# A decoder layer's attention rows through HBM: k rows stored once and read as three blocks, q rows written in three parts

## The chip, the cores and the metric

The kernel runs on one NeuronCore of one Trainium2 chip. The time is device microseconds of one execution; the kernel before was timed three times, with a median of 647.1 us (646.86 to 648.7). Everything shown here from inside an execution comes from one more, profiled execution. In this text TensorE (the matrix engine) is PE, VectorE is DVE, ScalarE is ACT and GpSimd is POOL; SP is the engine that issues nearly all DMAs.

## The reference, cut to what matters

The input is 16 batches of 128 rows of 128 features. Three blocks follow one another, each with 16 heads of 8 features: causal self-attention without projections, cross-attention with a bias of 16x16x128x128, and an attention block with a mixture of experts behind it.

```
def reference(x, ctx_1024, bias, ...):
    # self-attention: q = k = v = layernorm(x)
    w = einsum('bhqd,bhkd->bhqk', q, k) / sqrt(8);  w = where(causal, w, min)
    x = x + merge(softmax(w) @ v)
    # cross-attention: q from layernorm(x), k and v from ctx_1024
    scores = einsum('bhtd,bhsd->bhts', q, k) + bias
    x = x + merge(softmax(scores) @ v) @ Wo.T + bo
    # third block, on x = layernorm-ed input: attention with wq, wk, wv, wo,
    # then layernorm, argmax over 8 experts, relu(h @ w1[e] + b1[e]) @ w2[e] + b2[e]
    ...
```

## The kernel before, in words

The three layers (SELF, CROSS, FFN in the code) go over the 16 batches in pairs of two, so there are 24 pairs in all, numbered 0 to 23 here (SELF 0 to 7, CROSS 8 to 15, FFN 16 to 23). One head has only 8 features, and q and k are wanted to nearly float32 accuracy from bfloat16 matmuls. So q and k of a pair are each split into three bfloat16 parts (high, middle, low), and the product of all nine combinations of parts is one matmul with 9 x 8 = 72 rows: the tile `stack` holds on its 72 partitions the q rows (index 0) and the k rows (index 1) of a pair, for all 16 heads, 8192 bytes per row. Row r of q and row r of k must be the same feature, and over the 9 rows of a feature every q part meets every k part once.

The parts come out of ACT and POOL in the tile `parts`, whose partition is head by feature. To bring the features onto the partitions the rows go through scratch tensors in HBM:

- `write_parts` (L323) waits until POOL has written the low part (L501) and until the stack reads that used the same scratch buffer are done, and then issues one DMA of the q rows (L330, 192 KB) and three of the k rows (L335, 192 KB each). Each k DMA writes one part to three places, so `k_scratch` holds all 72 rows of k (576 KB); `q_scratch` holds 24 rows.
- `read_stack` (L338) waits until all four have landed (`WRITES`, L204) and until the first score group of the pair before is computed, so that the other stack buffer is free. Then it issues one DMA of the q rows (L346, every scratch row read three times) and one of the 72 k rows (L349).

SP works through its list in order. In each pair it reads the stack of the next pair, loads bias tiles (CROSS, `load_bias`, L351) and context rows (L364), and, one batch later, writes the parts of the pair after. `scores` and `score_maxes` on PE wait for the stack (semaphore `s_stack`); in CROSS and FFN `score_maxes` of the next pair is the first to do so, in the first batch of the pair before. All this runs through DMA queues that SP feeds. Behind the three layers come the routing and the 23 expert tiles, which the change does not touch.

## Time and profile before

| | us |
|---|---|
| median of 3 runs | 647.1 |
| the profiled execution | 649.13 |
| its span, first to last instruction | 647.4 |
| PE busy | 474.6 (73% of the span) |
| DVE busy | 295.2 (46%) |
| ACT busy | 216.3 (33%) |
| PE waiting for the stack rows (matmul side) | 88.1 |

The span is 1.7 us shorter than the execution's time. The three attention layers fill the first 500 us, the routing and the experts the rest. PE's busy time is a sum over overlapping matmuls, so 73% does not say that PE is the limit; what counts is where PE stands still and who ends the stillness.

### The profile page before, as it was taken

Reading aid. Unit: us, or ns where it says so; the run is one execution under the profiler, and the core shown is the slowest. Engines: PE = TensorE matmul, PEld = TensorE weight load, DVE = VectorE, ACT = ScalarE, POOL = GpSimd, SP = SyncE. Lnnn points to the kernel's source line nnn. Section 1 sums busy time; section 2 is a strip of 40 time slices with the busy share of each in tenths; the row PEclk is TensorE's granted clock in tenths of the full one; section 3 lists DMA queues with packets and bytes.
Section 4 is the critical chain, followed back from the end, with each engine's and each line's share of the span. In section 5 each row is a group of like instructions: output and inputs, shape, how many; then the busy total and the mean of one; then the engine's idle time right before and its main releaser. Section 6 shows DMA issues by size and latency. Waiting matters only on the chain.

```text
span 647.4 us, 15191 instructions
## 1 busy us (share of the span) xinstructions
PE 474.6 (73%) x4957; PEld 351.0 (54%) x4958; DVE 295.2 (46%) x1230; ACT 216.3 (33%) x415; POOL 131.2 (20%) x223
## 2 busy tenths in 40 slices
PE   0369669668988988987976956875785982058886
PEld 0246446446767777776765644554564761026664
DVE  4013223235756766675745635544544444014443
ACT  1136346433333343333233532432433330013331
POOL 4301112101011011111112111211202131713333
PEclk9968789768989999998979978967977555569999
DMA  6874565727687679575314224313328930222220
GB/s 181 235 191 114 162 170 136 190 73 175 153 196 181 163 185 222 150 184 139 86 38 123 57 68 121 95 46 103 107 53 230 345 120 0 106 69 53 72 67 19
DMA packets 95613, 83.82 MB, mean 129 GB/s; under 512 B 4934, under 2 KB 88905, under 8 KB 91993
## 3 DMA queue, kind: packets, MB, share of 16 engines
q1 hardware_dynamic: 94072, 80.20, 47.3%
q0 software_dynamic: 1504, 3.16, 1.4%
q8 instruction: 20, 0.33, 0.2%
q14 instruction: 17, 0.13, 0.1%
HBM read 58.29 MB, written 25.51 MB: 129 GB/s over the span
## 4 chain that ended last, share of the span: by engine, by line
PE 38%; DMA 24%; issue 17%; DVE 7%; POOL 6%; SPq 4%; ACT 2%; DVEq 0%; POOLq 0%; ACTq 0%
DMA stack<-k_scratch 19%; PE score_bank L582 13%; PE out_bank L582 7%; DMA k_scratch<-parts 4%; PE finish_bank L582 4%; PE prep_bank L582 3%; PE max_bank L582 3%; POOL routed_rows L559 2%; PE finish_bank L585 2%; SPq L335 2%; PE score_bank L585 2%; SPq L346 2%; PE max_bank L585 1%; POOL parts L501 1%; PE prep_bank L585 1%
## 5 line engine op out<-in xcount | busy, mean ns | idle before, releaser
L911 ACT ACTIVATE probs<-score_bank 128x512 f32<-128x512 f32 x192 | 115.0, 599 | 201.0 <-PE score_bank L582 200.7
L582 PE MATMUL score_bank<-stack 72*128 72x128 bf16 x768 | 143.1, 237 | 1.2 <-DVE maxT L1115 0.5
L582 PE MATMUL score_bank<-maxT,pick 128*128 128x128 bf16 x512 | 98.2, 230 | 0.0
L582 PE MATMUL max_bank<-stack 72*128 72x128 bf16 x512 | 55.5, 246 | 56.8 <-DMA stack<-k_scratch 56.1
L582 PE MATMUL out_bank<-probs,vaug 128*32 128x128 f32 x1536 | 90.1, 311 | 2.6 <-DVE vaug L1081 1.8
L582 PEld LDWEIGHTS score_bank<-stack 72*128 72x128 bf16 x768 | 83.6, 110 | 13.1 <-issue 8.8
L1093 DVE CUSTOM_DVE_ANT_0 max_bank<-max_bank,bias_in 128x128 f32<-128x128 f32 x256 | 66.2, 324 | 46.7 <-PE max_bank L582 46.2
L582 PEld LDWEIGHTS max_bank<-stack 72*128 72x128 bf16 x512 | 37.8, 109 | 72.3 <-issue 42.1
L1098 DVE TENSOR_REDUCE rowmax<-max_bank 128x4 f32<-128x512 f32 x64 | 43.4, 689 | 63.0 <-PE max_bank L582 62.7
L582 PE MATMUL score_bank<-causal,identb 128*128 128x128 bf16 x256 | 44.0, 249 | 32.0 <-DMA stack<-k_scratch 32.0
L501 POOL TENSOR_TENSOR parts<-rest,parts 128x512 bf16<-128x512 f32 (+1 forms) x24 | 23.9, 994 | 213.3 <-ACT parts L903 213.3
L585 PE MATMUL score_bank<-ident,bias_in 128*128 128x128 f32 x256 | 65.8, 290 | 1.0 <-DVE maxT L1115 0.2
L582 PEld LDWEIGHTS score_bank<-maxT,pick 128*128 128x128 bf16 x512 | 53.4, 104 | 3.4
L582 PEld LDWEIGHTS score_bank<-causal,identb 128*128 128x128 bf16 x256 | 27.2, 111 | 47.6 <-issue 47.3
L475 POOL TENSOR_SCALAR vareps<-meanvar 128x2 f32<-128x2 f32 x40 | 8.7, 218 | 210.8 <-DVE meanvar L1026 210.8
L1122 DVE RECIPROCAL rowsum_inv<-finish_bank 128x16 f32<-128x16 f32 x48 | 12.3, 256 | 80.1 <-PE finish_bank L585 80.1
L582 PEld LDWEIGHTS out_bank<-probs,vaug 128*32 128x32 f32 x1536 | 31.9, 114 | 28.9 <-issue 11.9
L585 PE MATMUL finish_bank<-ident,outT 128*128 128x128 f32 x203 | 37.4, 305 | 7.7 <-ACT outT L917 7.6
L585 PEld LDWEIGHTS score_bank<-ident,bias_in 128*128 128x128 f32 x256 | 36.6, 143 | 10.6 <-issue 6.5
L1303 DVE TENSOR_TENSOR probs<-score_bank,b_rows 128x512 f32<-128x512 f32 x23 | 15.9, 692 | 47.9 <-PE score_bank L582 47.9
L1093 DVE DVE_READ_ACCUMULATOR2_ANT rowmax<- 128x1 f32 x256 | 36.4, 142 | 0.0
L582 PE MATMUL finish_bank<-wxo,att_sel 128*128 128x128 f32 x256 | 34.9, 294 | 1.0 <-DVE att_sel L1129 0.5
(135 smaller groups left out, 706.9 us busy)
## 6 DMA issues: line engine op xcount, KB each, us to landing
bias_in<-in_bias SPq DMA_DIRECT2D x32, 512.0 KB, 9.1
k_scratch<-parts SPq DMA_DIRECT2D x72, 192.0 KB, 2.9
stack<-q_scratch SPq DMA_DIRECT2D x24, 576.0 KB
stack<-k_scratch SPq DMA_DIRECT2D x24, 576.0 KB
q_scratch<-parts SPq DMA_DIRECT2D x24, 192.0 KB, 2.7
routed_rows<-filler SPq DMA_DIRECT2D x1, 2955.5 KB, 20.4
w<-in_w SPq DMA_DIRECT2D x1, 2048.0 KB, 23.9
b_rows<-in_b SPq DMA_DIRECT2D x1, 2048.0 KB, 20.2
```

The source lines that it names most:

```text
L335: sp.dma_start(k_rows, parts[:, i, part, wk, :].unsqueeze(1).to_broadcast([128, NT, PAIR])).then_inc(s_wr[i], 16)
L346: sp.dma_start(stack[:, i, 0, :, :], q_src).then_inc(s_stack[i], 16)
L475: nc.gpsimd.tensor_scalar(vareps[:], meanvar[:, :, 1], EPS, None, ALU.add).then_inc(s_ve, 1)
L501: nc.gpsimd.tensor_tensor(parts[:, i, 2, 0:n, :], rest[:, 0:n, :], parts[:, i, 1, 0:n, :], ALU.subtract).then_inc(s_lo, 1)
L559: nc.gpsimd.indirect_dma_start(out=routed, out_offset=bass.IndirectOffsetOnAxis(ap=position_i[:, n:n + 1], axis=0), in_=rows_out[:, n, :], ...
L582: return nc.tensor.matmul(o, lhsT, rhs, start=start, stop=stop, **kw)
L585: return nc.tensor.matmul(o, src, ident[:], start=True, stop=stop, is_transpose=True)
L911: nc.scalar.activation(probs[:, g, :], sbk[g % 2][:], ACT.Exp, scale=1.0 if st.layer == CROSS else SCALE).then_inc(s_p, 1)
L1093: last = nc.vector.tensor_tensor_reduce(out=bank[:, h * S:(h + 1) * S], in0=bank[:, h * S:(h + 1) * S], in1=bias_in[:, k % 4, head, :], sc ...
L1098: last = nc.vector.tensor_reduce(rowmax[:, g * G:(g + 1) * G], bank[:].rearrange("p (h k) -> p h k", h=G), AX.X, ALU.max)
L1122: nc.vector.reciprocal(rowsum_inv[:], o[:, :, HD]).then_inc(s_inv, 1)
L1303: nc.vector.tensor_tensor(mid[:, k % 2, :], sbk[k % 2][:], b1_rows[:, bass.ds(e, 1), :].rearrange("p o f -> p (o f)"), ALU.add).then_inc(s ...
```

## The change

`k_scratch` loses the dimension that repeated each row three times: it has 24 rows (192 KB) now, feature by part, and one DMA writes them. `q_scratch` is ordered part by feature, so its rows are written by three DMAs of 64 KB, one per part. On the way back the q rows are still read by one DMA, each row three times in a row; the 24 k rows are read three times, by three DMAs, each into one block of 24 stack partitions. The number of stack rows and what stands on them in pairs is the same, in another order. So a pair writes 384 KB instead of 768 KB, and reads 1152 KB as before; it takes 8 DMA issues instead of 6.

```diff
-        q_scratch = nc.dram_tensor("q_scratch", (2, HD, NT, NH, PAIR), bf16, kind="Internal").ap()
-        k_scratch = nc.dram_tensor("k_scratch", (2, HD, NT, NT, NH, PAIR), bf16, kind="Internal").ap()
+        q_scratch = nc.dram_tensor("q_scratch", (2, NT, HD, NH, PAIR), bf16, kind="Internal").ap()
+        k_scratch = nc.dram_tensor("k_scratch", (2, HD, NT, NH, PAIR), bf16, kind="Internal").ap()
...
-        WRITES, READS = (1 + NT) * 16, 2 * 16
+        WRITES, READS = (1 + NT) * 16, (1 + NT) * 16
...
-                q_rows = bass.AP(tensor=q_scratch.tensor, offset=q_scratch[i].offset,
-                                 ap=[[PAIR, NH], [row_elems, HD * NT], [1, PAIR]])
-                sp.dma_start(q_rows, parts[:, i, :, 0, :]).then_inc(s_wr[i], 16)
                 wk = 0 if st.layer == SELF else 1
                 for part in range(NT):
-                    k_rows = bass.AP(tensor=k_scratch.tensor, offset=k_scratch[i, 0, 0, part].offset,
-                                     ap=[[PAIR, NH], [NT * row_elems, HD * NT], [1, PAIR]])
-                    sp.dma_start(k_rows, parts[:, i, part, wk, :].unsqueeze(1).to_broadcast([128, NT, PAIR])
-                                 ).then_inc(s_wr[i], 16)
+                    q_rows = bass.AP(tensor=q_scratch.tensor, offset=q_scratch[i, part].offset,
+                                     ap=[[PAIR, NH], [row_elems, HD], [1, PAIR]])
+                    sp.dma_start(q_rows, parts[:, i, part, 0, :]).then_inc(s_wr[i], 16)
+                k_rows = bass.AP(tensor=k_scratch.tensor, offset=k_scratch[i].offset,
+                                 ap=[[PAIR, NH], [row_elems, HD * NT], [1, PAIR]])
+                sp.dma_start(k_rows, parts[:, i, :, wk, :]).then_inc(s_wr[i], 16)
...
                 k_src = bass.AP(tensor=k_scratch.tensor, offset=k_scratch[i].offset,
-                                ap=[[row_elems, ROWS], [1, row_elems]])
-                sp.dma_start(stack[:, i, 1, :, :], k_src).then_inc(s_stack[i], 16)
+                                ap=[[row_elems, HD * NT], [1, row_elems]])
+                for rep in range(NT):
+                    sp.dma_start(stack[rep * HD * NT:(rep + 1) * HD * NT, i, 1, :, :], k_src).then_inc(s_stack[i], 16)
```

On PE, DVE, ACT and POOL the list of instructions is the same. SP's list at the start of the program, as a difference (a DMA's shape is its destination's, x3 is three of them; L358 are the first bias tiles):

```order
 L320 DMA gate_w<-in_gate_w 128x8
 L321 DMA gate_b<-in_gate_b 128x8
-L330 DMA q_scratch<-parts 16x24x256
-L335 DMA k_scratch<-parts 16x24x256 x3
-L346 DMA stack<-q_scratch 72x1x4096
-L349 DMA stack<-k_scratch 72x4096
+L332 DMA q_scratch<-parts 16x8x256 x3
+L335 DMA k_scratch<-parts 16x24x256
+L345 DMA stack<-q_scratch 72x1x4096
+L349 DMA stack<-k_scratch 24x4096 x3
```

Nothing has moved past anything else here: the four writes are one large one and three small ones now, the large one last, and two more reads stand before what follows. The same in the last step of SELF, where the context and bias loads of CROSS begin:

```order
 L364 DMA ctx_in<-in_ctx 128x2x128 x2
-L346 DMA stack<-q_scratch 72x1x4096
-L349 DMA stack<-k_scratch 72x4096
+L345 DMA stack<-q_scratch 72x1x4096
+L349 DMA stack<-k_scratch 24x4096 x3
 L358 DMA bias_in<-in_bias 128x8x128 x2
```

The bias loads come behind two more DMA issues.

## Rows read from the trace of the kernel before

**Rows 1.** Page, part 4: the chain that ended last, by line, share of the span.

```profile
DMA stack<-k_scratch 19%; PE score_bank L582 13%; PE out_bank L582 7%; DMA k_scratch<-parts 4%; PE finish_bank L582 4%; PE prep_bank L582 3%; PE max_bank L582 3%; POOL routed_rows L559 2%; PE finish_bank L585 2%; SPq L335 2%; PE score_bank L585 2%; SPq L346 2%; PE max_bank L585 1%; POOL parts L501 1%; PE prep_bank L585 1%
```

**Rows 2.** Waits: who waited for whom; us in total, times, longest us.

```profile
PE max_bank L582 <- DMA stack<-k_scratch: 56.1, 16, 6.9
PE score_bank L582 <- DMA stack<-k_scratch: 32.0, 5, 12.7
```

**Rows 3.** PE in order of time: start, us, what, [idle before, releaser].

```profile
161.35 0.61 PE L582 MATMUL max_bank<-stack 72*128 72x128 bf16 x8 [0.48 <-DMA stack<-k_scratch]
...
209.24 0.61 PE L582 MATMUL max_bank<-stack 72*128 72x128 bf16 x8 [1.21 <-DMA stack<-k_scratch]
...
424.48 1.04 PE L582 MATMUL max_bank<-stack 72*128 72x128 bf16 x8 [5.36 <-DMA stack<-k_scratch]
```

**Rows 4.** The chain, 194 to 210 us (pair 11): start, us, what.

```profile
194.53 1.17 POOL parts L501
...
195.72 0.56 SPq L330
...
196.33 0.62 SPq L335
...
197.68 2.88 DMA k_scratch<-parts
...
200.68 0.82 SPq L346
...
201.54 7.57 DMA stack<-k_scratch
...
209.24 0.61 PE max_bank L582 x8
```

**Rows 5.** SP's DMA issues by line: count, duration ns min/median/max, first and last start.

```profile
L330 SPq DMA_DIRECT2D q_scratch<-parts x24: 546/556/1128, 10.7 to 481.9; - x24
...
L335 SPq DMA_DIRECT2D k_scratch<-parts x72: 615/641/955, 11.4 to 483.8; - x72
...
L349 SPq DMA_DIRECT2D stack<-k_scratch x24: 516/528/540, 18.2 to 487.5; - x24
...
L407 SPq DMA_DIRECT2D outT<-routed_rows x23: 328/333/787, 570.6 to 629.4; - x23
```

**Rows 6.** Page, part 6: count, KB each, median us from issue to landing.

```profile
k_scratch<-parts SPq DMA_DIRECT2D x72, 192.0 KB, 2.9
...
q_scratch<-parts SPq DMA_DIRECT2D x24, 192.0 KB, 2.7
```

**Rows 7.** Stretches of the span; the last two columns are DMA share and GB/s.

```profile
core 0: us, PE busy (x) PEld busy (x) DVE busy (x) ACT busy (x) POOL busy (x), PEclk, DMA share, GB/s
...
372.20:378.00 5.80, 0.00 (x0) 0.00 (x0) 0.77 (x3) 0.00 (x0) 0.92 (x3) 0.84 0.69 189
...
203.00:208.00 5.00, 4.94 (x61) 3.71 (x59) 2.45 (x11) 2.40 (x5) 1.47 (x4) 1.00 0.90 233
...
435.50:438.70 3.20, 2.85 (x40) 1.85 (x39) 2.75 (x11) 0.68 (x2) 0.00 (x0) 1.00 0.95 243
504.00:512.00 8.00, 7.46 (x54) 6.25 (x55) 3.52 (x9) 3.02 (x6) 1.52 (x3) 0.50 1.07 357
```

**Rows 8.** The chain, 12 to 42 us (pairs 0 and 1): start, us, what.

```profile
12.77 4.54 DMA k_scratch<-parts
...
18.21 7.66 DMA stack<-k_scratch
...
31.34 10.34 DMA stack<-k_scratch
```

**Rows 9.** SP in order of time, 18 to 31 us: start, us, what.

```profile
21.45 8.08 SPq L358 DMA_DIRECT2D bias_in<-in_bias  x4
29.87 1.42 SPq L346 DMA_DIRECT2D stack<-q_scratch  x1
```

**Rows 10.** PE's weight loads in order of time, at 106.5 us (pair 6).

```profile
106.50 0.10 PEld L582 LDWEIGHTS score_bank<-causal,identb 128*128 128x128 bf16 x1 [0.26 <-DMA stack<-k_scratch]
```

## The prediction

> **What bounds the kernel now.** I read the chain of waits first. Its largest single piece is no engine but a transfer: the stack rows' read has 19% of the span and the writes of the k rows 4% [rows 1]. The list of waits says the same from PE's side: PE stood still 56.1 us, 16 times, before the row maxima of a new pair, and 32.0 us, 5 times, before scores, each time for the stack's read [rows 2]. In order of time one sees how long each such stop is: 0.48 us at pair 9, 1.21 us at pair 11, 5.36 us at pair 20; the other CROSS and FFN pairs lie between 1.2 and 6.9 us [rows 3]. So in nearly every pair PE is done early, and what sets the pair's length is a loop: POOL's low part, SP's four write issues, the last k write's landing, the two read issues, their landing, PE's work until the next low part [rows 4]. From the landing to the next low part PE works without a stop, so a microsecond less between the low part and the landing is a microsecond less per pair, until PE's stop is used up.
>
> The read is not late for another reason: the first score group of the pair before, the read's other wait, is ready some 5 us before the read's issue in pairs 9 to 23 and in 3, 5 and 7, by the start of the exponentials that follow it. In pairs 2, 4 and 6 it comes 1 us before the issue, about with the landing, so there the writes have nothing to give.
>
> **The writes.** Before, the first issue starts at 195.72 and the last of four at 197.68, 1.96 us later; it lands after 2.88 us more, so 4.84 us from first issue to last landing [rows 4]. Now three issues of 64 KB come first, and one of 192 KB last. No row shows the small one. The bounds are 0.33 us (a plain 64 KB load late in the program) and 0.64 us (the repeated k write) [rows 5]; I take 0.48, nearest to the q write's 0.556, whose shape it shares with a third of the pieces. With the gaps of 0.05 us that stand between issues, the k write is issued 3 x 0.53 = 1.6 us after the first. A 192 KB write with nothing queued in front landed in 2.7 us, the ones behind it in 2.9 [rows 6]. Sum 4.3 us, so **0.55 us gained** per pair. The ends: 3 x 0.38 + 2.7 = 3.8 us (1.0 gained) and 3 x 0.69 + 2.9 = 5.0 us (0.1 lost). The halved bytes by themselves give little here: SP's issues pace the writes, and the engines are only just behind (243 GB/s at a share of 0.95 [rows 7]).
>
> **The reads.** The q read is unchanged. The k read is three DMAs of 24 rows, with as many bytes and as many rows of 8192 bytes. Issuing three takes 2 x (0.53 + 0.05) = 1.15 us longer [rows 5], but issue is not what the read waits for: from the k issue to the landing it is 7.57 us [rows 4], in which 1152 KB go at 189 GB/s with a share of 0.69 [rows 7], so the q rows alone keep the engines busy for about 3 us and the last k issue comes 2 us after the first read issue, in time. What it costs depends on what the 189 GB/s are limited by. A stretch in which bias tiles are loaded beside the read has 233 GB/s, and the experts' weights came with 357 [rows 7], so it is neither the HBM nor the engines as a whole; the rate belongs to this transfer, to its 72 rows. With 24 rows at a time it may be the same or lower. The low end is no cost, or 0.3 us gained (192 KB of source instead of 576; the landings vary by as much). The high end is far: 10.34 us was measured for a k read in company of bias loads, 2.7 us above the 7.66 of the one before [rows 8]. I take **0.5 us lost** per read, nearer to the low end since bytes, rows and the order in which engines get them stay, and under half of the 1.15 us by which the last issue moves.
>
> The Trainium skill has a rule that speaks against the change: in "SBUF — State Buffer", section "Door 1: The DMA port swizzle", a transfer's rate is the number of ports that its partitions reach times 27.2 GB/s, and partitions 0 to 63 reach only eight of sixteen. By it 24 partitions reach six ports, an estimate of 163 GB/s, 3.6 us for 589,824 bytes. The 189 GB/s of the 72 rows [rows 7] fit its eight ports and a little, so the trace agrees as far as it goes; the k half takes 3.1 us at 189 GB/s, the rule's cost is 0.5 us, and no row here shows a transfer to 24 partitions.
>
> **The sum.** Pairs 3, 5, 7, 8 and 9 to 23 have both terms on the path: 19 x (-0.55 + 0.5) = -1.0 us. Pair 9, with a stop of 0.48, can't give more than that, which the sum does not feel.
>
> At the start the writes of pair 0 queue behind the weights' loads: their last landing takes 4.54 us instead of 2.9 [rows 6, 8]. Here the bytes count: 384 KB less at 243 GB/s is 1.6 us, less 0.5 for the read: -1.1. Pair 1's read stands behind four bias issues, which take 8.08 us since their queue is full of pair 0's read and pair 1's writes [rows 9]; the same bytes leave that queue, the same 0.5 is paid: -1.1 again.
>
> Pairs 2, 4 and 6 have their read released by PE, and its landing is just in time (a weight load of pair 6 stood 0.26 us for it [rows 10]). They pay the 0.5 us less a small slack: I take 0.2 each, +0.6. Bias and context loads come 1.15 us later from SP. Their cover is that a bias tile is asked for three batches ahead; without it PE would lose that 1.15 us at most once per pair.
>
> Total -1.0 - 2.2 + 0.6 = **-2.6 us**. The profiled execution took 649.13 us, 2.0 above the median of 647.1, so I take the difference off the median: **644.5 us**. The own range of this case, with the per-pair net between -0.35 and +0.3, is 638 to 650. A measurement of this kernel can tell about 0.3%, 1.9 us, from no change.
>
> **The rivals.**
> 1. The read is not slower at all. Speaking for it: same bytes, same number of rows, queue never empty. Against: that the rate belongs to the 72 rows, which become 24. Then 19 x -0.55 = -10.5, at the start -3.2, pairs 2, 4, 6 nothing: -13.7, about 633.5 us. Chance 0.22.
> 2. Slower: the three blocks of 24 rows go at three quarters of the present rate, 142 instead of 189 GB/s, so the k half takes 4.1 instead of 3.1 us. The point from which it decides is a cost of 0.65 us per read. Then 19 x (1.0 - 0.55) = +8.6, pairs 2, 4, 6 with 0.8 each +2.4, the start -1.2: +9.8, 657 us. For it: a third of the partitions, and the loss falls on every pair's loop. Against: the engines still have the same rows each. Chance 0.24.
> 3. The writes give nothing: the small q writes cost 0.64 us each in SP like the k writes, so the last is issued at 2.07 us instead of 1.96, and lands as late as before. For it: the issue cost in the rows does not follow the bytes (0.53 us for 576 KB, 0.64 for 192 [rows 5]). With 0.5 us for the read: +9.5, the start -1.0, the rest +0.6: +9, 656 us. Chance 0.12.
>
> **How the numbers follow.** The forecast has 0.42; within it somewhat more than half lies below -1.9 us (0.24), a third within (0.13), the rest above (0.05). Rival 1 is faster (0.22). Of rivals 2 and 3 a quarter lies within 0.3% (0.09) and the rest is slower (0.27). So faster 0.46, same 0.22, slower 0.32. The range runs from rival 1's time to rival 2's, 634 to 657, and leaves the outer halves of both out.
>
> **What would show it.** In the profile after: the distance from the first write issue to the k write's landing is 4.3 us (3.8 if issues are cheap, 4.9 if rival 3 holds). From the last k read's issue to its landing, plus 1.15 us, against 7.57 us: 8.1 in all for me, 7.6 for rival 1, 8.6 for rival 2; the stretch's GB/s falls in its second half only. PE's waits for the stack stay at about 86 us. The write's stretch has half the bytes. I am wrong in kind, not only in size, if the read's release comes from PE's scores in most pairs, or if a bias tile becomes what PE waits for.

## The result, and the profile after

| | before | after |
|---|---|---|
| median of 4 runs each, same chip | 646.98 us | 656.75 us |
| lowest and highest | 640.36, 648.7 | 653.44, 658.32 |
| the profiled execution | 649.13 | 653.44 |
| its span | 647.4 | 651.7 |

The ratio is 1.0164, 95% interval 1.0082 to 1.0245: the change makes the kernel slower by about 10 us. Forecast were 644.5 us, 2.6 less than before. Medians here and below are over all executions, while the ratios leave out executions over 1.5% above the fastest of the same kernel, so that the two can differ by up to 1%. The profiled execution of after is the fastest of its four, 3.3 us under their median. So the two traces differ by only 4.3 us, and part of the work is to see why.

The chain of waits after, by line (answers to [rows 1]), and the two waits of PE for the stack (answers to [rows 2]):

```profile
DMA stack<-k_scratch 14%; PE score_bank L582 10%; PE out_bank L582 6%; DMA k_scratch<-parts 4%; PE finish_bank L582 4%; PE prep_bank L582 3%; PE max_bank L582 3%; SPq L332 3%; POOL routed_rows L559 2%; PE finish_bank L585 2%; SPq L349 2%; POOL parts L501 2%; PE score_bank L585 2%; PE max_bank L585 1%; SPq L345 1%
```

```profile
PE max_bank L582 <- DMA stack<-k_scratch: 66.6, 16, 9.5
PE score_bank L582 <- DMA stack<-k_scratch: 27.0, 5, 11.6
```

The waits before the maxima grew from 56.1 to 66.6 us, those before the scores, which are all at the start and in SELF, fell from 32.0 to 27.0; together they are 93.6 us, where the prediction had about 86. The read's share of the chain fell from 19% to 14%, which isn't a gain, as the waits show: 23% of this chain is time in which the engine waited for nothing that the profile shows, and the steps have to be measured one by one. The loop of one pair (pair 13; answers to [rows 4]; start, us, what):

```profile
245.91 1.17 POOL parts L501
247.09 0.55 SPq L332
247.69 0.59 SPq L332
248.32 0.60 SPq L332
248.96 2.78 DMA k_scratch<-parts
...
251.86 0.82 SPq L345
252.73 0.53 SPq L349
253.30 0.36 SPq L349
253.70 7.13 DMA stack<-k_scratch
260.97 0.74 PE max_bank L582 x8
```

SP's issues by line (count, duration ns min/median/max, first and last start; answers to [rows 5]), and the landings (answers to [rows 6]):

```profile
L332 SPq DMA_DIRECT2D q_scratch<-parts x72: 536/598/1265, 10.8 to 491.7; - x72
L335 SPq DMA_DIRECT2D k_scratch<-parts x24: 599/600/611, 12.7 to 492.3; - x24
L349 SPq DMA_DIRECT2D stack<-k_scratch x72: 342/366/1529, 16.8 to 498.1; - x72
```

```profile
q_scratch<-parts SPq DMA_DIRECT2D x72, 64.0 KB, 2.1
k_scratch<-parts SPq DMA_DIRECT2D x24, 192.0 KB, 2.8
```

A q write of a third of the bytes holds SP for 0.598 us; the one of 192 KB before held it for 0.556. Sorted by place in the list this difference turns round: the first of the four write issues of a pair takes 0.546 us with 64 KB (after) and 0.556 with 192 KB (before), the next two 0.60 in after (64 KB) and 0.63 to 0.64 in before (192 KB, repeated; medians of 24 pairs). The k write is issued at 248.96, 1.87 us after the first issue, where it was 1.96 before and the prediction had 1.6.

The read, first while its q half and then while its k half is on its way; the last three columns are PE's granted clock, DMA share and GB/s (answers to [rows 7]). Before:

```profile
348.00:351.00 3.00, 2.15 (x33) 1.34 (x33) 2.04 (x10) 1.46 (x3) 0.71 (x1) 1.00 0.71 210
351.00:353.80 2.80, 0.66 (x4) 0.42 (x4) 1.23 (x6) 0.66 (x2) 1.44 (x4) 1.00 0.65 170
```

After:

```profile
355.00:358.00 3.00, 2.08 (x35) 1.27 (x33) 2.20 (x8) 1.13 (x3) 0.93 (x2) 1.00 0.78 221
358.30:361.60 3.30, 0.71 (x5) 0.42 (x4) 1.30 (x6) 0.74 (x2) 1.79 (x4) 1.00 0.64 139
```

The q half is as it was. The k half, the same 589,824 bytes, goes at 139 instead of 170 GB/s, at the same share of the engines: they are as busy and move less. (The view counts a packet's bytes where it starts, so part of the k half falls into the first stretch. Over all 24 reads the packets of the k half take 3.57 instead of 3.12 us, see below, which is 165 instead of 189 GB/s.)

**Where the time went.** POOL's low part marks the pairs. The one of pair 9 and that of pair 23, before and after:

```profile
145.91 1.15 POOL L501 TENSOR_TENSOR parts<-rest,parts 128x512 bf16<-128x512 f32 x1 [15.44 <-ACT parts L903]
...
480.69 1.15 POOL L501 TENSOR_TENSOR parts<-rest,parts 128x512 bf16<-128x512 f32 x1 [12.06 <-ACT parts L903]
```

```profile
147.79 1.16 POOL L501 TENSOR_TENSOR parts<-rest,parts 128x512 bf16<-128x512 f32 x1 [18.27 <-ACT parts L903]
...
489.25 1.16 POOL L501 TENSOR_TENSOR parts<-rest,parts 128x512 bf16<-128x512 f32 x1 [12.00 <-ACT parts L903]
```

At pair 9 after is 1.9 us behind, at pair 23 it is 8.6 us behind. The 14 pairs between (6.7 us) can be cut into three pieces each, from the rows of SP, PE and POOL in order of time: from the first write issue to the read issue; from there to PE's first maxima of the new pair; from there to the end of the next low part. Between a low part's end and the first write issue there are 0.03 to 0.12 us, which only the last column holds. Summed over the 14 pairs, in us:

| | writes | read | PE piece | whole |
|---|---|---|---|---|
| before | 71.7 | 124.0 | 138.2 | 334.8 |
| after | 66.7 | 133.3 | 140.5 | 341.5 |
| difference | -5.0 | +9.3 | +2.3 | +6.7 |

The +9.3 of the read are all in its k half: from the last packet of the q half to the last of the k half the 14 reads take 53.8 instead of 44.8 us. The time to the first packet, the q half and the time from the last packet to PE's start differ by 0.5 us or less.

Then the difference is given back, but not by the change. From the low part of pair 23 on no new pair is waited for, and the work up to the routing takes this long, before and after (the column ahead of the last two is PE's granted clock):

```profile
480.70:548.60 67.90, 48.50 (x402) 35.68 (x394) 32.16 (x112) 20.56 (x42) 14.20 (x26) 0.58 0.58 175
```

```profile
489.20:551.10 61.90, 39.79 (x405) 29.53 (x402) 32.45 (x112) 20.57 (x42) 14.24 (x26) 0.73 0.61 185
```

The instructions are the same, and in before PE is granted 0.58 of its clock, in after 0.73: 6.0 us. In the profiled executions of the other kernels the stretch took 60 to 68 us (55.9 in one), with either way of writing (67.8 in k_first below, with after's writes, 62.1 in split_read, with before's), and on the whole longer the lower the granted clock was. So it doesn't follow the change; that it is chance from one execution to the next is likely, but each kernel has only one trace. 1.9 + 6.7 - 6.0, and 1.8 us in the routing and experts, which the change doesn't touch, are the 4.3 us between the two spans; the medians show the 8.6 and a little more.

### The profile page after: what moved, and what is told of

Its sections match the earlier page's. It is cut to its first block, busy times and chain, and to the rows that moved or that the text cites. A ratio compares the mean times of both kernels' runs of the same rounds, so it can differ in the third digit from the quotient of the medians.

```text
span 651.7 us, 15239 instructions
## 1 busy us (share of the span) xinstructions
PE 471.6 (72%) x4957; PEld 348.8 (54%) x4958; DVE 295.5 (45%) x1230; ACT 216.9 (33%) x415; POOL 131.5 (20%) x223
## 4 chain that ended last, share of the span: by engine, by line
PE 34%; issue 23%; DMA 19%; POOL 7%; DVE 7%; SPq 6%; ACT 3%; DVEq 0%; POOLq 0%; ACTq 0%
DMA stack<-k_scratch 14%; PE score_bank L582 10%; PE out_bank L582 6%; DMA k_scratch<-parts 4%; PE finish_bank L582 4%; PE prep_bank L582 3%; PE max_bank L582 3%; SPq L332 3%; POOL routed_rows L559 2%; PE finish_bank L585 2%; SPq L349 2%; POOL parts L501 2%; PE score_bank L585 2%; PE max_bank L585 1%; SPq L345 1%
## 5 line engine op out<-in xcount | busy, mean ns | idle before, releaser
L582 PE MATMUL score_bank<-stack 72*128 72x128 bf16 x768 | 140.6, 234 | 1.6 <-DVE maxT L1115 1.0
L582 PE MATMUL max_bank<-stack 72*128 72x128 bf16 x512 | 54.7, 244 | 67.2 <-DMA stack<-k_scratch 66.6
L582 PE MATMUL score_bank<-maxT,pick 128*128 128x128 bf16 x512 | 94.2, 222 | 0.0
L582 PE MATMUL out_bank<-probs,vaug 128*32 128x128 f32 x1536 | 88.7, 306 | 2.8 <-DVE vaug L1081 1.8
L582 PEld LDWEIGHTS score_bank<-stack 72*128 72x128 bf16 x768 | 82.2, 108 | 12.6 <-issue 8.0
L582 PE MATMUL score_bank<-causal,identb 128*128 128x128 bf16 x256 | 45.4, 254 | 27.3 <-DMA stack<-k_scratch 27.0
L585 PE MATMUL score_bank<-ident,bias_in 128*128 128x128 f32 x256 | 64.1, 284 | 1.3 <-DVE maxT L1115 0.4
L582 PEld LDWEIGHTS score_bank<-maxT,pick 128*128 128x128 bf16 x512 | 51.3, 100 | 3.0
L582 PEld LDWEIGHTS out_bank<-probs,vaug 128*32 128x32 f32 x1536 | 31.7, 113 | 28.4 <-issue 11.4
L585 PEld LDWEIGHTS score_bank<-ident,bias_in 128*128 128x128 f32 x256 | 35.8, 140 | 10.5 <-issue 5.9
L582 PEld LDWEIGHTS finish_bank<-wxo,att_sel 128*128 128x128 f32 x256 | 36.6, 223 | 3.4 <-DVE att_sel L1129 2.4
L582 PE MATMUL finish_bank<-wxo,att_sel 128*128 128x128 f32 x256 | 37.7, 309 | 1.0 <-DVE att_sel L1129 0.5
```

The source lines that it names most:

```text
L582: return nc.tensor.matmul(o, lhsT, rhs, start=start, stop=stop, **kw)
L585: return nc.tensor.matmul(o, src, ident[:], start=True, stop=stop, is_transpose=True)
```

## The experiments

Each was timed beside the kernel before on the same chip; the ratios are to before, with 95% intervals. Three chips were used beside that of the result: before's own median was 647.69 us beside split_read, writes_only, stride3 and spread28, 645.57 beside k_first, base12, after_spread28 and spread_kfirst, and 648.64 beside the last three to be tried (warm, spread_kfirst_warm, halves). So differences of some 2 us between medians of different groups say nothing. The last four columns are the sums of the table above as differences to before, from one profiled execution each; that one can lie off its kernel's median (base12's took 632.32 us, 5 above).

| kernel | median us | ratio | writes | read | PE piece | whole |
|---|---|---|---|---|---|---|
| after | 656.75 | 1.016 (1.008 to 1.024) | -5.0 | +9.3 | +2.3 | +6.7 |
| split_read | 658.72 | 1.025 (1.017 to 1.033) | -2.6 | +9.2 | +5.1 | +11.7 |
| writes_only | 648.58 | 1.007 (1.001 to 1.013) | -4.4 | +6.6 | +3.0 | +5.2 |
| k_first | 637.92 | 0.988 (0.984 to 0.992) | -14.4 | +7.9 | -3.2 | -9.7 |
| stride3 | 636.98 | 0.989 (0.983 to 0.994) | -4.3 | -2.8 | -2.1 | -9.2 |
| spread28 | 612.51 | 0.953 (0.945 to 0.961) | -2.1 | -11.7 | -9.1 | -22.9 |
| base12 | 627.06 | 0.968 (0.961 to 0.975) | -2.2 | -6.2 | -0.8 | -9.1 |
| after_spread28 | 627.48 | 0.975 (0.968 to 0.982) | -4.9 | +1.4 | -3.8 | -7.3 |
| warm | 637.03 | 0.980 (0.974 to 0.987) | -2.0 | +2.5 | -11.9 | -11.4 |
| spread_kfirst | 609.83 | 0.944 (0.939 to 0.949) | -14.4 | -1.1 | -6.0 | -21.5 |
| spread_kfirst_warm | 605.02 | 0.941 (0.935 to 0.946) | -14.1 | +1.8 | -12.5 | -24.8 |
| halves | 586.87 | 0.912 (0.908 to 0.917) | -0.7 | -36.1 | 0.0 | -36.5 |

Kernels with before's own writes show -2.0 to -2.6 in the column of the writes (halves, whose reads are other ones, -0.7). Two reads of before were issued late in its profiled execution (pair 10 by 0.6 and pair 18 by 2.0 us). Delays of that kind are rarer elsewhere (0.7 in warm, 0.5 in stride3, 1.7 in halves). So about 2.2 us of most numbers of that column belong to before's two.

### The read alone, in three blocks

```diff
-                k_src = bass.AP(tensor=k_scratch.tensor, offset=k_scratch[i].offset,
-                                ap=[[row_elems, ROWS], [1, row_elems]])
-                sp.dma_start(stack[:, i, 1, :, :], k_src).then_inc(s_stack[i], 16)
+                for rep in range(NT):
+                    k_src = bass.AP(tensor=k_scratch.tensor, offset=k_scratch[i].offset + rep * HD * NT * row_elems,
+                                    ap=[[row_elems, HD * NT], [1, row_elems]])
+                    sp.dma_start(stack[rep * HD * NT:(rep + 1) * HD * NT, i, 1, :, :], k_src).then_inc(s_stack[i], 16)
```

> The kernel before with one edit: the 72 k rows, still stored 72 times, are read by three DMAs into three blocks of 24 stack partitions. Writes as before. Theory 1 (a block of 24 partitions takes fewer bytes per microsecond than 72, because fewer ways into SBUF lead to it): the read takes about 0.6 us longer per pair, as in the changed kernel, the release of the read after the first write issue stays at 4.9 us, and the time is slower than before by some 20 x 0.6 = 12 us. Theory 2 (the read of the changed kernel is slower because it reads the same 24 scratch rows three times): no change in the read, time as before.

Measured: 658.72 us, 11 us slower than before's median and 2.5% by the ratio; the interval overlaps that of after. Its read costs 9.2 us over the 14 pairs, 0.66 each, like after's 9.3. It has before's writes, so this is the price of reading into three blocks; whether it is their number or their place, stride3 asks below. Its windows (q half, k half):

```profile
431.80:434.80 3.00, 1.28 (x16) 0.86 (x12) 1.67 (x8) 1.31 (x3) 1.06 (x3) 1.00 0.78 213
...
435.00:438.50 3.50, 0.00 (x0) 0.00 (x0) 0.00 (x0) 0.00 (x0) 0.53 (x2) 0.55 0.61 131
```

The k half is the slow one again (131 GB/s), though here it reads 72 stored rows: where the bytes come from doesn't matter.

### The writes alone

The writes of after; the k read is one DMA to all 72 partitions that takes each of the 24 rows three times in a row, as the q read does. The kernel leaves out the right pairing of q and k parts, so it computes something else in the same number of steps.

```diff
                 k_src = bass.AP(tensor=k_scratch.tensor, offset=k_scratch[i].offset,
-                                ap=[[row_elems, HD * NT], [1, row_elems]])
-                for rep in range(NT):
-                    sp.dma_start(stack[rep * HD * NT:(rep + 1) * HD * NT, i, 1, :, :], k_src).then_inc(s_stack[i], 16)
+                                ap=[[row_elems, HD * NT], [0, NT], [1, row_elems]])
+                sp.dma_start(stack[:, i, 1, :, :], k_src).then_inc(s_stack[i], 16)
```

> The changed kernel's writes (three q writes of 64 KB, one k write of 192 KB), with the k rows read by one DMA, each scratch row three times in a row as the q rows are. The products then pair only equal parts of q and k, three times over, so the output is not the reference's. Theory 1: the read is as fast as before (about 8.3 us from its first issue to landing), and only the gain of the writes is left: 0.15 to 0.2 us per pair and some 2 us at the start, so 3 to 6 us faster than before. Theory 2 (reading the same rows again is what is slow): the read takes 0.6 us longer as in the changed kernel, the time is that of the changed kernel.

Measured: 648.58 us, 1.007 of before. The writes' piece is 4.4 us shorter over 14 pairs, or 2.2 without the two late reads of before: 0.16 per pair, where 0.55 was forecast. But the read that I had taken for neutral isn't: it costs 6.6 us. Its k half:

```profile
396.40:399.40 3.00, 2.07 (x28) 1.35 (x26) 1.81 (x9) 1.57 (x3) 0.92 (x2) 1.00 0.84 218
399.40:403.10 3.70, 0.00 (x0) 0.00 (x0) 0.52 (x2) 0.00 (x0) 0.86 (x2) 0.93 0.46 135
```

135 GB/s, but at a share of 0.46, where after has 139 GB/s at 0.64. A packet of the k half takes 0.51 us on average, as in before, against 0.59 in after; but at the end a few engines are still at work when the others are done: for a median of 0.59 us at most four packets are on their way (0.19 in before, 0.25 in after). So here the last packets are late, and in after all of them are slow. Why they are late no run shows. So this run doesn't give the writes' worth by its time, only by its piece.

### The k write first

```diff
                 wk = 0 if st.layer == SELF else 1
+                k_rows = bass.AP(tensor=k_scratch.tensor, offset=k_scratch[i].offset,
+                                 ap=[[PAIR, NH], [row_elems, HD * NT], [1, PAIR]])
+                sp.dma_start(k_rows, parts[:, i, :, wk, :]).then_inc(s_wr[i], 16)
                 for part in range(NT):
...
-                k_rows = bass.AP(tensor=k_scratch.tensor, offset=k_scratch[i].offset,
-                                 ap=[[PAIR, NH], [row_elems, HD * NT], [1, PAIR]])
-                sp.dma_start(k_rows, parts[:, i, :, wk, :]).then_inc(s_wr[i], 16)
```

> The changed kernel with the four writes in another order: the large k write (192 KB) is issued first, the three q writes (64 KB) behind it. Theory (the write term came out small since each small q write costs SP 0.6 us of issue, so the large k write stands at 1.9 us and lands 2.8 us later): a q write lands 2.1 us after its issue, so the last landing comes at 1.9 + 2.1 = 4.0 instead of 4.7 us after the first issue, 0.7 us less on each pair's loop, 10 to 14 us faster than the changed kernel and about even with the kernel before. Rival (the landings are bound by the bytes in the queue, not by the last issue): the release of the read stays at 4.7 us, the time is the changed kernel's.

Measured: 637.92 us, 18.8 less than after (0.988 of before where after has 1.016), and 1.2% faster than before, by the same four writes in another order. SP in order of time, of this kernel and then of after:

```profile
426.01 0.56 SPq L331 DMA_DIRECT2D k_scratch<-parts  x1
426.61 1.92 SPq L335 DMA_DIRECT2D q_scratch<-parts  x3
430.11 0.81 SPq L345 DMA_DIRECT2D stack<-q_scratch  x1
```

```profile
443.27 1.83 SPq L332 DMA_DIRECT2D q_scratch<-parts  x3
445.14 0.60 SPq L335 DMA_DIRECT2D k_scratch<-parts  x1
448.00 0.81 SPq L345 DMA_DIRECT2D stack<-q_scratch  x1
```

The issues take as long, and the 192 KB write, first now, holds SP for 0.557 us (median), where it took 0.600 as the last. The last one carries 64 KB instead of 192, and these land in 2.1 us instead of 2.8: from first issue to the read 4.10 us instead of 4.73, and over the 14 pairs 57.3 instead of 66.7 us.

### Which partitions a DMA writes

Four kernels ask why the block of 24 rows is slow. stride3 is after, with block `rep` going to every third partition of the 72 (it, too, leaves out the right pairing of q and k rows):

```diff
-                    sp.dma_start(stack[rep * HD * NT:(rep + 1) * HD * NT, i, 1, :, :], k_src).then_inc(s_stack[i], 16)
+                    sp.dma_start(stack[rep:ROWS:NT, i, 1, :, :], k_src).then_inc(s_stack[i], 16)
```

> The changed kernel with each of the three k reads going to every third stack partition (0, 3, ..., 69 and so on) instead of to 24 adjacent ones. The row pairing is then wrong, so the output is not the reference's; number, size and source of the DMAs are the changed kernel's. Theory 1 (the destination's 24 adjacent partitions are the cost): the read is as fast as before, the time is 3 to 6 us below before. Rival (three DMAs instead of one cost the time, by their issues or their ends): the read stays 0.6 to 0.7 us longer, the time is the changed kernel's, about 10 us above before.

spread28 is before, with the stack on partitions 28 to 99 instead of 0 to 71; the 28 below are zeroed once, and PE's matmuls have 100 rows:

```diff
+BASE = 28
...
-        stack = sb("stack", [ROWS, 2, 2, NH, PAIR], bf16)
+        stack = sb("stack", [BASE + ROWS, 2, 2, NH, PAIR], bf16)
...
-                sp.dma_start(stack[:, i, 0, :, :], q_src).then_inc(s_stack[i], 16)
+                sp.dma_start(stack[BASE:, i, 0, :, :], q_src).then_inc(s_stack[i], 16)
...
-                sp.dma_start(stack[:, i, 1, :, :], k_src).then_inc(s_stack[i], 16)
+                sp.dma_start(stack[BASE:, i, 1, :, :], k_src).then_inc(s_stack[i], 16)
...
+            nc.vector.memset(stack[0:BASE, :, :, :, :], 0.0).then_inc(s_zero, 1)
```

> The kernel before with the stack on partitions 28 to 99 instead of 0 to 71, the 28 rows below are zeroed once by DVE; the matmuls take 100 rows of which 28 are zero. Issues and bytes are the kernel before's. Theory 1 (the rate of the stack read is set by how many ways into SBUF its partitions reach: half of the rows now lie above partition 63): the rate of the read rises from 190 GB/s towards 300, the read takes 1.5 to 2.3 us less per pair, and the time falls by 25 to 40 us. Rival (the rate is set by the source in HBM or by 12 engines as such): same read, same time as before, or a little more for the zeroing.

base12 is the same with `BASE = 12` (partitions 12 to 83):

> The kernel before with the stack on partitions 12 to 83: 52 rows below partition 64 and 20 above, where the kernel before has 64 and 8, and the stack on partitions 28 to 99 has 36 and 36. Twelve rows of zeros in the matmuls. If the fuller half sets the read's rate, the read takes between the two measured ones, 6.3 and 5.7 us, near 6.0, and the time lies some 10 to 15 us below the kernel before. If what helped at 28 was something that starts only when both halves are equal, or the alignment, the time is that of the kernel before.

after_spread28 is after with `BASE = 28`, its three blocks on 28 to 51, 52 to 75 and 76 to 99:

> The changed kernel with the stack on partitions 28 to 99. The q read is one DMA to 72 partitions in both halves, the k reads are still three blocks of 24 adjacent partitions. Theory (width: the rate of a DMA follows the number of ways that its own partitions reach, wherever they lie): the q half of the read takes 2.7 us as on 28 to 99 before, the k half stays at 3.6 us; the time falls by less than it did for the kernel before, some 10 us below the changed kernel. Rival (place: it is the load on the lower half that counts): the k half falls too, to under 3.1 us, and the time comes near the 612 us of the kernel before so moved.

Measured, with the time that the packets of a read take in the trace (q half: from the first packet's start to the end of the 72nd; k half: from there to the end of the last; medians of the 24 reads):

| kernel | q half | k half | median us |
|---|---|---|---|
| before (72 rows on 0 to 71) | 3.14 | 3.12 | 647 |
| after (k in blocks of 24) | 3.18 | 3.57 | 656.75 |
| split_read | 3.14 | 3.69 | 658.72 |
| stride3 (k on every third) | 3.13 | 3.02 | 636.98 |
| base12 (12 to 83) | 2.83 | 2.92 | 627.06 |
| spread28 (28 to 99) | 2.74 | 2.95 | 612.51 |
| after_spread28 | 2.63 | 3.56 | 627.48 |

stride3 has after's writes and after's three DMAs of 24 rows, and its k half is as fast as before's. So it is neither three DMAs nor 24 rows that cost, but 24 adjacent partitions; nor does the last issue's time matter, which in stride3 is later still (2.40 us after the read's first issue, 1.83 in after). Its 637 us are 11 below before's median, 1.1% by the ratio, and more than the 3 to 6 expected. Moving the whole stack makes the 72-row reads faster and leaves the blocks at 3.56. Windows of spread28 (q half, k half) and of the k half of after_spread28:

```profile
330.40:333.00 2.60, 1.69 (x29) 1.01 (x29) 1.80 (x8) 0.98 (x2) 0.76 (x2) 1.00 0.69 243
333.20:335.50 2.30, 0.96 (x10) 0.54 (x7) 1.29 (x7) 0.99 (x3) 0.93 (x2) 1.00 0.63 196
```

```profile
428.90:432.00 3.10, 0.00 (x0) 0.00 (x0) 0.58 (x2) 0.00 (x0) 0.86 (x2) 1.00 0.58 132
```

243 and 196 GB/s against 210 and 170 before, at the same share, and 132 for a block that stands on 28 to 99 against 139 on 0 to 71. The theories held for the reads, the times went further than expected: spread28 is within its 25 to 40 us, but base12 is 18 us below before (10 to 15 expected) and after_spread28 29 below after (10 expected). Of these 29 the 14 pairs hold 14, and 12 were gained up to pair 9; more than the q half's 0.5 us per read is in them, the PE pieces among it (-3.8 against +2.3).

The Trainium skill's page "SBUF — State Buffer", section "Door 1: The DMA port swizzle", gives each partition one of sixteen ports, from its number. By its table each block of 24 in after reaches six ports, and so does each in after_spread28, though 28 to 99 as a whole reach all sixteen: the 3.57 and 3.56 agree with that, and the estimate for six ports was 3.6 us. It also names the ports of the others: ten for 0 to 71 and for every block of stride3, thirteen for 12 to 83, sixteen for 28 to 99. The order of the measured q halves (3.14, 2.83, 2.74) agrees, the size doesn't: by 27.2 GB/s for a port, ten would be 2.2 us and sixteen 1.4 us by that estimate, and 3.1 and 2.6 to 2.7 were measured. The prediction gave the 72 rows "eight ports and a little", where the table has ten. The runs show that the set of partitions decides; that it does so through ports is the page's reading, and no run separates it from another property of the same sets. Nothing here shows what else limits the read. In every kernel such a DMA ends with twelve packets of 4 bytes, and mostly twelve of its packets are on their way at once, so it seems to be carried by 12 of the 16 engines.

### PE's clock after a stop

The PE piece has no wait for a DMA in it, and yet it changes by up to 12.5 us. The first maxima after the stop, in after (pairs 9, 11 and 20), and in the kernel of this section (pair 21; start, us, what, [idle before, releaser]):

```profile
163.27 0.61 PE L582 MATMUL max_bank<-stack 72*128 72x128 bf16 x8 [2.35 <-DMA stack<-k_scratch]
...
213.62 1.01 PE L582 MATMUL max_bank<-stack 72*128 72x128 bf16 x8 [2.35 <-DMA stack<-k_scratch]
...
433.92 1.03 PE L582 MATMUL max_bank<-stack 72*128 72x128 bf16 x8 [6.19 <-DMA stack<-k_scratch]
```

```profile
435.72 3.29 PE L583 MATMUL max_bank<-causal,identb 128*128 128x128 bf16 x56
...
440.21 0.62 PE L583 MATMUL max_bank<-stack 72*128 72x128 bf16 x8 [1.21 <-DMA stack<-k_scratch]
```

warm is before with 56 matmuls on constants ahead of the wait for the stack in FFN, into a bank that is overwritten anyway:

```diff
+                if g == 0 and k % 2 == 0 and st.layer == FFN:
+                    for _ in range(WARM):
+                        mm(bank[:, 0:S], identb[:], causal[:])
```

> The kernel before with 56 matmuls of constants (128 columns each, into a bank that is overwritten next) put on PE just ahead of its wait for the stack, once per pair of the third layer, where PE stands still for 4.8 us on average. They take about 3.3 us at the full clock and nothing else changes. Theory (part of what a microsecond of loop costs is TensorE's clock: after a long stop the granted clock falls and PE's work until the next low part takes 10.0 us instead of 9.1): the granted clock in the third layer rises from 0.84 and that piece falls towards 9.3 us, some 5 us in all over 8 pairs; write and read pieces stay. Rival (the clock has no part, the differences between runs are chance): no change, or slower where the stop is shorter than 3.3 us.

Measured: 637.03 us, about 12 less than before where 5 had been expected, by work that is of no use. The granted clock in FFN, before and in warm (third number from the end):

```profile
320.00:488.00 168.00, 124.60 (x1405) 90.65 (x1404) 84.76 (x260) 60.96 (x121) 27.70 (x52) 0.84 0.31 83
```

```profile
320.00:488.00 168.00, 144.01 (x1926) 112.31 (x1925) 92.37 (x289) 64.15 (x127) 30.56 (x56) 0.97 0.39 102
```

PE is granted 0.97 instead of 0.84 of full speed. After the long stop the eight maxima take 1.03 us (the level of 1.2 GHz), after the matmuls and a stop of 1.21 us they take 0.62 (2.4 GHz). The piece from PE's start to the next low part has a median of 7.5 instead of 9.8 us in FFN. In pairs 9 to 14 (CROSS) it takes 8.95 us or 10.5 in before and after and nothing between. Pairs 9 and 10 of before, with the same 109 matmuls:

```profile
161.35:170.30 8.95, 8.87 (x109) 7.09 (x109) 6.52 (x38) 3.96 (x9) 1.16 (x1) 1.00 0.68 175
185.16:195.69 10.53, 10.45 (x109) 8.46 (x109) 5.45 (x37) 3.73 (x8) 1.16 (x1) 0.85 0.62 158
```

The short piece was granted 1.00 of the clock, the long one 0.85. Before has one slow one in the six pairs from 9 on, after a stop of 2.68 us, the longest of the six; after has three, with stops of 3.93, 2.35 and 1.55 us. The stop's length alone doesn't decide: the same 2.35 us was followed by 0.61 and by 1.01 us. But in these two kernels longer stops go with more slow returns, and then a microsecond of read time costs more than one. How much more varies: base12 took 8.4 us out of writes and read and its PE pieces lost only 0.8.

### The parts together

spread_kfirst is after with `BASE = 28` and the k write first, both as above:

> The changed kernel with both edits: the stack on partitions 28 to 99 and the k write issued before the three q writes. The two act on different pieces of the same loop, so their gains should add: 0.7 us from the writes and 0.4 from the q half of the read, 20 us below the changed kernel. Against the kernel before with the stack moved (612 us) it has the read 0.6 us longer and the writes 0.9 us shorter, and 2 us less at the start: 605 to 612 us. If the q writes' landing is not the last one, the gain is only the read's.

spread_kfirst_warm adds the constant matmuls of warm, 36 of them:

> The version with the stack on partitions 28 to 99 and the k write first, with 36 matmuls of constants (about 2.1 us) ahead of the same wait in the third layer, where PE still stands 3.4 us. If the clock matters there as in the kernel before, 2 to 5 us below that version's 610 us; if its clock is already up (0.88 granted), no change.

halves is spread28 with each read cut by heads: q and k of heads 0 to 7 first, then of 8 to 15 with a semaphore of their own, which PE waits for only at its third group.

```diff
+                half = row_elems // 2
+                for upper in range(2):
+                    heads, done = slice(upper * NH // 2, (upper + 1) * NH // 2), (s_stack, s_upper)[upper][i]
+                    q_src = bass.AP(tensor=q_scratch.tensor, offset=q_scratch[i].offset + upper * half,
+                                    ap=[[row_elems, HD * NT], [0, NT], [1, half]])
+                    sp.dma_start(stack[BASE:, i, 0, heads, :], q_src).then_inc(done, 16)
+                    k_src = bass.AP(tensor=k_scratch.tensor, offset=k_scratch[i].offset + upper * half,
+                                    ap=[[row_elems, ROWS], [1, half]])
+                    sp.dma_start(stack[BASE:, i, 1, heads, :], k_src).then_inc(done, 16)
...
-                if g == 0:
-                    wait(pe, s_stack[k // 2 % 2], st.turn(k // 2) * READS + READS)
+                if g % 2 == 0:
+                    wait(pe, (s_stack, s_upper)[g // 2][k // 2 % 2], st.turn(k // 2) * READS + READS)
```

> The kernel before with the stack on partitions 28 to 99, and the read in two steps: q and k rows of heads 0 to 7 first, then of heads 8 to 15, each with its own semaphore; PE waits for the second only at its third group. Rows are 4096 bytes. Theory (what counts per pair is the time until PE can begin, not the bytes): PE begins after half of the bytes, about 2 us earlier on each pair's loop, and the time falls well below the 612 us of that version, to 575 to 595 us. Rival (rows of half the length or the two more issues cost as much as is gained, or PE then waits for the second half): the time is within 1% of 612 us.

Measured: 609.83, 605.02 and 586.87 us. With the stack moved, after's edit with the k write first gains at most 2.7 us over spread28 itself (612.51), which the two intervals don't separate, since its read is the slower one: -14.4 for the writes and -1.1 for the read, where spread28 has -2.1 and -11.7. The constant matmuls bring 4.8 us more by the medians; here, too, the intervals overlap, and what the trace shows is the PE piece (-12.5 instead of -6.0). halves keeps before's four writes and is the fastest: its waits and its chain in one pair of FFN,

```profile
PE max_bank L589 <- DMA stack<-k_scratch: 26.3, 15, 6.1
PE score_bank L589 <- DMA stack<-k_scratch: 7.6, 4, 2.5
```

```profile
352.00 0.80 SPq L353
352.85 0.52 SPq L356
353.42 0.81 SPq L353
354.27 5.13 DMA stack<-k_scratch
```

33.9 us of waits instead of 88.1. From the read's issue to PE's start there are 5.4 us in FFN, 7.5 in spread28 and 8.6 in before (medians), since PE needs half the bytes to begin. That is 26 us of the kernel's time beside spread28, whose own gain is 35. The version that beats both kernels by most is this one, at 0.912 of before; k write first inside it was not tried.

## Why the prediction was wrong

It had the bound right: nearly every pair is that loop, and both terms of the change fall on it. It had the sign of each term right too, and the time lies just inside its range of 634 to 657. But a small gain was forecast and a loss came. Their sum was to be about nothing (-0.55 + 0.5 per pair), and a sum of two terms that nearly cancel has no sign to rely on.

**The writes: the step that failed.** "No row shows the small one ... I take 0.48": the 64 KB write takes SP 0.598 us. The term was taken from the q write's 0.556, "whose shape it shares", but the low price goes with a place in the list and not with a shape or size: the first write issue of a pair takes 0.546 us in after (64 KB), 0.556 in before and 0.557 in k_first (192 KB), the later ones 0.60 or more. So the k write is issued 1.87 us after the first instead of 1.6, and lands 2.8 us after that (2.7 had been taken): 4.7 instead of 4.3. The gain is 0.18 us per pair (4.73 against 4.91 from first write issue to read issue in FFN), not 0.55. This is near what rival 3 said (0.64 us per issue, no gain), which had a chance of 0.12 and a time of 656 us. The rows pointed there: in [rows 5] the issues of 576 KB take 0.53 us and those of 192 KB 0.56 and 0.64, and the lower bound of 0.33 us is an issue of another form.

**The read: right in kind, somewhat small.** 0.5 us was taken; it is 0.67 by the table, 0.66 in split_read, which has nothing else. All of it is the k half's packets. By the medians they take 0.45 us longer (3.57 against 3.12), near the 0.5 that the prediction worked out from the Trainium skill's rule for six ports ("SBUF — State Buffer", "Door 1: The DMA port swizzle"); the rest comes from a few long ones, above all that of pair 10 (5.41 us instead of 3.32). The later last issue has no part: in stride3 it is later still and the read loses nothing. Rival 1 (no cost) falls with split_read. Rival 2 had 657 us nearly to the point, by luck: its price of 1.0 us per read is shown by no run, and its time came out by a write that gains less and a clock that it didn't have.

**The sum.** By the measured terms a pair loses 0.48 us, over 14 pairs 6.7. The table has 6.7 as well, made up otherwise (9.3 - 5.0, of the latter 2.2 from before's two late reads) and 2.3 of PE's clock. Over the prediction's 19 pairs the terms make 9; the medians differ by 9.8. (The own range was added up slightly low: with +0.3 per pair its upper end is 651 us, not 650.)

**The start: right.** PE's first start on the stack moved from 26.00 to 24.88 us, the second from 41.81 to 39.64: -1.1 and -2.2, as forecast.

**SELF: wrong in size.** Pairs 2, 4 and 6 were to pay 0.2 each. At pair 9 after is 1.9 us behind instead of 2 ahead. Pair 2's read took 9.0 us from its last issue, at 45.28, to its landing, PE stood 1.84 us for it, and from there the waits fall on the other pairs of each two: PE waits at 54.30, 82.88 and 108.94, where before waited at 69.55, 95.79 and 122.63. Pair 2's read is slow in each kernel that reads into blocks of 24 on 0 to 71 (its packets take 8.2 us in after, 8.3 in split_read, 7.9 in k_first) and not in before and stride3 (6.0 both). That it started the rest is argued from the rows, and no run isolates it.

**The clock: missing.** The prediction took a microsecond of the loop for a microsecond of time, 19 times. k_first shortens after's loop by 0.64 us per pair and the kernel by 18.8 us, 29 for each. Pairs count 22 at most; most of the rest is that PE comes back at a higher clock, and warm shows that part alone. Between after and k_first the PE pieces differ by 5.5 us, of which 4.3 are those of pairs 15 and 16, on the way into FFN (12.9 and 12.9 us at a granted clock of 0.74, 11.5 at 0.85 and 10.0 at 1.00). In FFN behind them k_first gained nothing. So a term for the clock belongs into the sum wherever a stop's length changes, with a wide range: its size isn't set by the stop alone.

## What to carry to other kernels

When a transfer is split, price it by the partitions that each piece writes, not only by its bytes or rows; and put what lands slowest first among several writes that one reader waits for. An issue time read from a row belongs to its place in the list as well. A term for which no row exists, in a sum near zero, decides the sign: give its least favourable nearby row (here the 0.64 us of the neighbouring write) more weight. Where PE waits for a transfer, ask how much of it the first consumer needs: half the bytes first was worth 26 us here, on top of the 35 of the moved stack.

## What the runs showed of the hardware

- The same 72-row read to partitions 28 to 99 instead of 0 to 71 moves 243 instead of 210 GB/s in its first half. The kernel gains 35 us by it, though PE's matmuls take 100 rows instead of 72: a score matmul takes 219 to 221 ns at the full granted clock and 314 at half of it in both kernels.
- Three DMAs of 24 rows to every third partition cost nothing against one of 72 (3.02 and 3.12 us); to 24 adjacent ones 3.57.
- The first of four write issues in a row holds SP for 0.55 to 0.56 us, with 64 or 192 KB (0.60 in halves, where SP has one semaphore more to wait for ahead of it); the later ones take about 0.60, and 0.63 to 0.65 with a repeated source.
- A DMA that repeats its source rows, behind another such, had a share of 0.46 in its stretch, with a few of its packets late; a plain one behind it had 0.65 (before).
- Four of after's reads (pairs 2, 10, 19 and 23) took 7.6 to 8.6 us in packets instead of 6.8. In two of these pairs one of SP's issues at L349 took 1.28 and 1.53 us (10 and 23) instead of 0.37. Their cause stays open.
- With no wait in it at all, the same stretch of work took 61.9 or 67.9 us by the clock that PE was granted (0.73 or 0.58). A single execution of this kernel can't tell 6 us from nothing in a comparison of totals; the pieces of a pair can.
